# Two hops of graph attention on one Trainium2 core: the table work between the hops in several lots at once, and 64 gathers of the second hop moved there

## The reference

```python
def _hop(emb, head, tail, rel_e, W, N):
    a_input = jnp.concatenate([emb[head], emb[tail]], axis=-1)
    e = jnp.sum(a_input @ W * rel_e, axis=-1)
    e = jax.nn.leaky_relu(e, NEG_SLOPE)
    seg_max = jax.ops.segment_max(e, head, num_segments=N)
    ex = jnp.exp(e - seg_max[head])
    denom = jax.ops.segment_sum(ex, head, num_segments=N)
    alpha = ex / denom[head]
    agg = jax.ops.segment_sum(emb[tail] * alpha[:, None], head, num_segments=N)
    return agg + emb
...
for _ in range(N_HOPS):          # 2
    emb = _hop(emb, head, tail, rel_e, W, N)
    emb = emb / jnp.maximum(jnp.linalg.norm(emb, axis=-1, keepdims=True), 1e-12)
    res = 0.5 * res + emb
...
return _layernorm(x + res, axis=-1)
```

## Time and profile before

| | before |
|---|---|
| median of 3 runs | 5809.42 us (5805.15 to 5809.52) |
| profiled execution | 5806.54 us |
| its span, first to last instruction | 5804.8 us |
| granted TensorE clock, mean | 0.694 |
| busy: PE / DVE / ACT / POOL | 52% / 73% / 20% / 58% |
| sort and preparation | up to 1004 us |
| first hop's loop | 1004 to 3253 |
| stage between the hops | 3253 to 3447 |
| second hop's loop | 3447 to 5687 |
| last stage | 5687 to 5805 |

### The profile page before, as it was taken

The page is one execution under the profiler, slowest core; times in us unless marked ns, Lnnn a source line. Parts: engine busy times, 40 slices in busy tenths (PEclk is TensorE's granted clock), DMA queues, the critical chain, the costliest instruction groups (busy, mean ns, idle before and its releaser), DMA issues. The chain is left out here.

```text
span 5804.8 us, 102013 instructions
## 1 busy us (share of the span) xinstructions
PE 3025.6 (52%) x23525; PEld 2371.0 (41%) x23525; DVE 4227.0 (73%) x14510; ACT 1184.5 (20%) x4455; POOL 3349.3 (58%) x3535
## 2 busy tenths in 40 slices
PE   4411100566666665555666555656656656666661
PEld 1111100445544454444455324544545444454451
DVE  8899998677677776767767436777777677776777
ACT  3310000112222122121221331221212212122122
POOL 0000000777777777777777117777777777777770
PEclk9755555677677777777767557777777777777775
DMA  2000001222222222222222212222222222222223
GB/s 62 0 0 0 0 0 38 58 54 53 57 53 53 53 54 56 54 53 54 56 54 53 38 32 54 53 57 54 53 57 54 53 53 53 57 53 53 54 48 67
DMA packets 234922, 269.99 MB, mean 47 GB/s; under 512 B 140893, under 2 KB 149309, under 8 KB 234550
## 3 DMA queue, kind: packets, MB, share of 16 engines
q0 software_dynamic: 112640, 115.57, 10.2%
q1 hardware_dynamic: 121910, 151.13, 8.6%
HBM read 253.57 MB, written 12.88 MB: 46 GB/s over the span
## 5 line engine op out<-in xcount | busy, mean ns | idle before, releaser
L625 POOL DMA_INDIRECT G<-rows,ixs x3520 | 3343.3, 950 | 2301.7 <-DVE ixs L793 1229.6
L791 DVE SCALAR_TENSOR_TENSOR acc<-acc,aS,psY 65x128 f32 x3520 | 1206.7, 343 | 814.0 <-PE psY L689 553.8
L640 PE MATMUL psX<-PT,oht 128*128 x3532 | 945.7, 268 | 1240.1 <-DVE logit L752 1095.1
L689 PE MATMUL psY<-G,wr 128*65 128x128 f32 x7040 | 1305.4, 318 | 166.4 <-DVE acc L791 143.6
L752 DVE CUSTOM_DVE_ANT_0 junk<-psX,G 128x192 f32<-128x192 f32 x3520 | 1158.0, 346 | 276.0 <-DMA G<-rows,ixs 229.5
L640 PEld LDWEIGHTS psX<-PT,oht 128*128 128x128 bf16 x3532 | 411.5, 116 | 1523.0 <-issue 1507.6
L689 PEld LDWEIGHTS psY<-G,wr 128*65 128x65 f32 x7040 | 910.3, 165 | 257.7 <-issue 221.0
L643 PE MATMUL psX<-v2lo,oht 128*128 128x128 bf16 x3532 | 955.0, 270 | 0.0
L642 PE MATMUL psX<-v,oht 128*128 128x128 bf16 x3532 | 953.5, 270 | 0.0
L641 PE MATMUL psX<-PTlo,oht 128*128 x3532 | 933.8, 264 | 0.0
L716 ACT ACTIVATE wr<-G,wS 128x64 f32<-128x64 f32 x3520 | 863.0, 334 | 0.0
(11 more groups left out here) (165 smaller groups left out, 2186.8 us busy)
## 6 DMA issues: line engine op xcount, KB each, us to landing
tb<-types_lin SPq DMA_DIRECT2D x222, 512.0 KB
G<-rows,ixs POOLq DMA_INDIRECT x3520, 2.4
emb<-rows SPq DMA_DIRECT2D x14, 448.0 KB, 6.9
mt<-marks_d SPq DMA_DIRECT2D x110, 48.1 KB
rows<-xin SPq DMA_DIRECT2D x1, 3136.0 KB, 16.2
rows<-emb SPq DMA_DIRECT2D x14, 224.0 KB, 2.4
res<-rows SPq DMA_DIRECT2D x7, 448.0 KB, 6.9
out_dram<-res SPq DMA_DIRECT2D x13, 224.0 KB
```

The costliest lines, as they stand in the source:

```text
L625: nc.gpsimd.indirect_dma_start(G[:, p, u, L:L + D], None, tab[hop], bass.IndirectOffsetOnAxis(ap=ixs[:, p, u:u + 1], axis=0)).then_inc(gat ...
L640: nc.tensor.matmul(x[:, 0:L], piece, PT[:, bass.ds(first, L)], start=True, stop=False)
L689: nc.tensor.matmul(psY[:, v % 8, :], wr[:, v // 16, v % 16, :], G[:, pq, v, 0:L], start=True, stop=True).then_inc(y_ok, 1)
L791: nc.vector.scalar_tensor_tensor(spot, spot, aS[:, pq, v:v + 1], psY[:, v % 8, :], ALU.mult, ALU.add).then_inc(acc_ok, 1)
```

## The change

Five things change, all around the stage between the hops.

1. **Order of the table work.** Each lot's table work is cut into pieces (`turn`, `product`, `first`, `second`). A list, the same for PE and ACT, mixes the pieces of neighbouring lots: product t, turn t+1, second t-1, first t, and so on. Behind rows(0) to rows(2) comes no piece, behind a later rows(g) one (g divisible by 3) or two, and behind rows(13) all the rest. ACT does its share of the pieces of g behind square and root of lot g.
2. **Gathers between the hops.** POOL gets a program in this stage: when all 14 stores have landed, it issues the 64 gathers of the next hop's groups 0 and 1. DVE copies both groups' row numbers at the stage's start. In the second hop POOL starts at group 2.
3. **The nodes' rows lie in G.** G, `ixs` and `acc` are allocated once. The lots' old and new rows stand in columns 0 to 63 (lots 0 to 6) and 64 to 127 (lots 7 to 13) of G's 64 slots, so that the gathers can fill columns 128 to 191 beside them. `emb` is gone, and `res` exists in the last stage alone.
4. **Loads by single lots**: 224 KB each and a semaphore each, in both stages, instead of 448 KB for two lots.
5. **`acc` is cleared** for the second hop at the end of DVE's work in the stage between, no longer at the hop's front.

```diff
@@ the hop loop, POOL and DVE
-                        if not logits:
+                        if not logits or (hop and not reached(g, 2)):
                             return
...
-                        if logits:
+                        if logits and (not hop or reached(g, 1)):
                             nc.vector.tensor_copy(ixs[:, 1 - p, :], ix[:, bass.ds(CG * g + CG, CG)]).then_inc(ix_ok, 1)
...
-                    nc.vector.tensor_copy(ixs[:, 0, :], ix[:, 0:CG]).then_inc(ix_ok, 1)
+                    if not hop:
+                        nc.vector.tensor_copy(ixs[:, 0, :], ix[:, 0:CG]).then_inc(ix_ok, 1)
                     dve.wait_ge(cst, hop + 1)
                     nc.vector.memset(srow[:, :], NEG)
-                    link(nc.vector.memset(acc[:, :], 0.0))
+                    if not hop:
+                        link(nc.vector.memset(acc[:, :], 0.0))
@@ the stage on the nodes
+                spots = G[:, :, :, :].rearrange("l p u w -> l (p u) w")
+
+                def rows_of(b0, b1):
+                    assert b0 // (NB // 2) == (b1 - 1) // (NB // 2)
+                    side = b0 // (NB // 2)
+                    return spots[:, b0 - side * NB // 2:b1 - side * NB // 2, side * D:(side + 1) * D]
+
+                def lot(g):
+                    return rows_of(g * NG, (g + 1) * NG)
...
+                def table_work():
+                    order = [("turn", 0)]
+                    for t in range(NS + 1):
+                        if t < NS:
+                            order.append(("product", t))
+                        if t + 1 < NS:
+                            order.append(("turn", t + 1))
+                        if t:
+                            order.append(("second", t - 1))
+                        if t < NS:
+                            order.append(("first", t))
+                    at = 0
+                    for g in range(NS):
+                        n = 0 if g < 3 else (1 if g % 3 == 0 else 2)
+                        yield g, order[at:at + n]
+                        at += n
+                    yield NS, order[at:]
...
-                    for k in range(NS // 2):
-                        two = slice(2 * k * NG, 2 * (k + 1) * NG)
-                        sp.dma_start(emb[:, two, :], tv[:, two, :]).then_inc(e_in[k], 16)
+                    for g in range(NS):
+                        sp.dma_start(lot(g), tv[:, part(g), :]).then_inc(e_in[g], 16)
...
+                if not final:
+                    @block.gpsimd
+                    def _(gp):
+
+                        gp.wait_ge(ix_ok, NGRP + 3)
+                        gp.wait_ge(tabw, 16 * NS)
+                        for p in range(2):
+                            for u in range(CG):
+                                nc.gpsimd.indirect_dma_start(
+                                    G[:, p, u, L:L + D], None, tab[1], bass.IndirectOffsetOnAxis(ap=ixs[:, p, u:u + 1], axis=0)).then_inc(gath[p][u // 8], 16)
...
-                    for g in range(NS):
-                        rows(g)
-                        if not final and g >= 2:
-                            table(g - 2)
-                            first_off(g - 2)
-                            second_off(g - 2)
-                    if not final:
-                        for g in (NS - 2, NS - 1):
-                            table(g)
-                            first_off(g)
-                            second_off(g)
+                    if final:
+                        for g in range(NS):
+                            rows(g)
+                    else:
+                        for g, work in table_work():
+                            if g < NS:
+                                rows(g)
+                            for kind, t in work:
+                                {"turn": turn, "product": product, "first": first_off, "second": second_off}[kind](t)
...
+                        for g, work in table_work():
                             if g < NS:
-                                square(g, g, emb)
+                                square(g, lot(g))
                                 root(g, g, 1)
-                            if g > 1:
-                                tables_out(g - 2)
-                    if not final:
-                        tables_out(NS - 1)
+                            for kind, t in work:
+                                {"turn": turned_out, "product": high, "first": middle, "second": low}[kind](t)
...
+                    if not final:
+                        nc.vector.tensor_copy(ixs[:, :, :].rearrange("l p u -> l (p u)"), ix[:, 0:2 * CG]).then_inc(ix_ok, 2)
...
                             if g < NS:
                                 sum_up(g, g, 1.0, 1e-24, ALU.max)
+
+                        link(nc.vector.memset(acc[:, :], 0.0))
```

More of the change, by code:

```diff
@@ L494, in gnn_kernel @@
             "sc_ok", "y_ok", "acc_ok"))
-        e_in = [sem(f"e_in{k}") for k in range(NB // 14)]
+        e_in = [sem(f"e_in{k}") for k in range(NB // 7)]
         n_tr, nrow, nsq, nsum, nroot, rooted, e_new, T_new, eT_new, m_new, m2_new, m3_new, hi_new, mid_new, p_new, tabw, n_out, y_out = (sem(n) for n in (
@@ L501, in gnn_kernel @@
         hop_at = {"n": 0}
+        G = sb(ctx, "G", [L, 2, CG, L + D])
+        ixs = sb(ctx, "ixs", [L, 2, CG], i32)
+        acc = sb(ctx, "acc", [V, WIDE])
         USES = [-(-NGRP // 2), NGRP // 2]
@@ L833, in _ @@
                             sp.wait_ge(e_new, g + 1)
[L834 removed]
+                            sp.dma_start(tab[1].rearrange("(b p) d -> p b d", p=L)[:, part(g), :], lot(g)).then_inc(tabw, 16)
                         else:
@@ L853, in rows, with turn @@
                         last.then_inc(n_tr, 1)
-                    def table(g):
+                    halves = (slice(0, 4 * L), slice(4 * L, NG * L))
+                    def turn(g):
                         pe.wait_ge(e_new, g + 1)
@@ L873, in first_off @@
                         pe.wait_ge(hi_new, g + 1)
-                        for w in (slice(0, 4 * L), slice(4 * L, NG * L)):
+                        for w in halves:
                             last = nc.tensor.matmul(psQ[:, g % 2, w], lessb[:, :], PT[:, cols(g)][:, w], start=False, stop=True, skip_group_check=True)
@@ L909, in tables_out, with high, middle, low @@
                         nc.scalar.copy(eTn[:, g % 2, :, :], psE[:, 0:NG, :]).then_inc(eT_new, 1)
+                    def high(g):
                         act.wait_ge(m_new, g + 1)
                         nc.scalar.copy(PT[:, cols(g)], psQ[:, g % 2, 0:NG * L]).then_inc(hi_new, 1)
+                    def middle(g):
                         act.wait_ge(m2_new, g + 1)
+                        if g >= 2:
+                            act.wait_ge(m3_new, g - 1)
                         nc.scalar.copy(midn[:, g % 2, :], psQ[0:T, g % 2, 0:NG * L])
                         nc.scalar.copy(PT[T:2 * T, cols(g)], psQ[T:2 * T, g % 2, 0:NG * L]).then_inc(mid_new, 1)
+                    def low(g):
                         act.wait_ge(m3_new, g + 1)
                         nc.scalar.copy(PTlo[0:T, cols(g)], psQ[0:T, g % 2, 0:NG * L]).then_inc(p_new, 1)
-                    for g in range(NS + 1):
-                        if final:
+                    if final:
+                        for g in range(NS + 1):
                             if g:
-                                square(g - 1, lots0 + 2 * g - 1, res)
+                                square(lots0 + 2 * g - 1, res[:, part(g - 1), :])
                             if g < NS:
-                                square(g, lots0 + 2 * g, emb)
+                                square(lots0 + 2 * g, lot(g))
                             if g:
```

63 lines of the change are left out of this document (30 added, 33 removed).

## The result

| | before | after |
|---|---|---|
| median | 5808.11 us (4 runs, 5805.15 to 5809.52) | **5714.9 us** (4 runs, 5712.45 to 5716.19) |
| ratio | | 0.9843, 95% interval 0.9831 to 0.9855 |
| profiled execution, its span | 5806.54, 5804.8 | 5716.12, 5714.2 |
| granted TensorE clock, mean | 0.694 | 0.698 |

A forecast was written before the change was run, and what follows sets the result against it. GpSimd's unbroken gathers were taken to bound the kernel, so gather 65's start sets the time: 93.5 us earlier plus 2.2 in the last stage, 95.7 off 5806.5, plus 2.9 for the median, gives 5713 us; range 5695 to 5745.

The forecast's parts named there:

- leaving the stage: End of the stage between the hops: all engines meet 0.3 us after the last gather; 3 more if waiting for landing.
- types, to the one-hots: Second hop's start: VectorE's one-hots wait 5.0 us for the 512 KB of types, bounds 3.0 and 13.6.
- Rows first: Stage between hops: lots wait for fewer table pieces, bare ones 3.24 us; last new rows at 3316.9 instead of 3416.6.
- The tables' tail: 38 table pieces left after the rows: about 7.1 us a lot, ending at 3385, hidden by gathers with 15 us spare.
- 5733 rival: Tail of the tables does not overlap, each lot keeps 10.74 us, stage ends at 3420, 20 us later; chance 0.10.
- Rows that wait for the tables: Stage between hops: each lot stays at 13.52 us, gather 65 starts at 3535, no change, 5813; chance 0.03.
- Gathers that do not run early: Stage ends at 3385 and 64 gathers follow; gather 65 near 3466, 31 us later, 5744; chance 0.05.
- What the gathers run beside: 64 gathers between the hops, beside ScalarE's casts and the memset: priced at nothing; 10.6 us if the memset held them.
- 5702 case: Stage between hops: PE's clock rises to 2.4 GHz with closer-packed work, saving 11 us; chance 0.12.
- The steps set the rate: Second hop: each us a step exceeds 40.07 is paid by 53 groups; 5766 at 41.1; chances 0.05 to 41.9, 0.03 beyond.
- last step case: Second hop: steps of 42.3 us, a loss of 118 against the gain, 5835, slower than before; steps beyond 41.9 chance 0.03.
- The last stage: Last stage: loads halved from 448 KB to 224 KB, so VectorE waits 2.2 us less than 5.34.

The follow-up runs named there:

- e2_gathers_alone: Kernel after, but with the old order of table pieces, all four of lot g-2 behind rows(g): 5817.14 us, ratio to before 1.0017.
- e1_order_alone: Kernel after without GpSimd's program between the hops; the second hop gathers groups 0 and 1 itself: 5738.85 us, ratio to before 0.9877.
- e6_tables_last: Kernel after with no table piece between the rows, all 56 behind rows(13): 5705.18 us, ratio to before 0.9827.
- e5_clear_in_hop: Kernel after, but acc is cleared at the second hop's front again: 5725.12 us, ratio to before 0.9859.
- e4_forty: Kernel after with 40 gathers between the hops, the other 24 at the second hop's front: 5692.93 us, ratio to before 0.9801.
- e8_seven_of_eight: Kernel after without every eighth gather from group 2 of the second hop on, those slots keeping older rows: 5629.88 us, ratio 0.9696.
- e3_probe_end: Kernel after; behind its 64 gathers GpSimd writes a small tile, waits for all to land, writes another: 5717.32 us in one execution.
- e10_forty_late_exit: The kernel with 40 gathers between the hops; GpSimd then waits for the tables' last cast and writes one small tile: 5694.44 us, one execution.
- e7_write_only: Kernel after without gathers between the hops; GpSimd there waits for the tables' last cast and writes one small tile: 5733.05 us, one execution.
- e9_writes64: The kernel with one small write and no gathers between the hops, but with 64 one-element writes: 5738.86 us in one execution.

## Why the prediction was right, step by step

Gather 65 was put at 3435.0 and came at 3436.87. Term by term, measured less predicted, in us:

| term | measured | predicted | difference |
|---|---|---|---|
| lot 1 starts | 3259.16 | 3258.6 | +0.6 |
| lots 1 to 13 | 50.5 | 53.2 | -2.7 |
| lot 13 to the last new rows | 4.6 | 5.1 | -0.5 |
| landing of the stores, wake-up | 3.2 | 2.9 | +0.3 |
| 64 gathers | 79.6 | 80.1 | -0.5 |
| **leaving the stage** | **5.5** | **0.3** | **+5.2** |
| types, to the one-hots | 4.0 | 5.0 | -1.0 |
| step 0 | 17.5 | 17.6 | -0.1 |
| step 1, to gather 65 | 12.7 | 12.25 | +0.5 |
| sum | | | +1.8 |

- **The mechanism held.** Everything moved with gather 65, one for one, in all eleven kernels that keep the whole computation.
- **The mis-sized term** is "Leaving the stage": the 0.3 was given without a row; the moment beside it, from the earlier trace rows, is the end of a stage in which GpSimd had nothing to do, so it could not hold a price for leaving after gathers. The bound above it, 3 us for landing, was too low and named the wrong cause. That the time came out within 2 us is luck in part: the rows' phase and the types, 2.7 and 1.0 shorter than priced, paid back 3.7 of the 5.2.
- **Rows first.** The forecast form was right lot by lot, with each of these lots 0.3 to 0.75 shorter than priced: lot 4 took 6.95 (7.7), lot 5 5.0 (5.5), lot 8 7.0 (7.6), lot 10 5.6 (5.85), lot 11 3.3 (3.9).
- **The tables' tail** had its 15 us to spare: 16.6, at 6.91 a lot (7.1). The 5733 rival falls.
- **Two rivals were built.** Rows that wait for the tables (5813) are e2_gathers_alone, which took 5817.14: the 5.2 that leaving the stage took beyond its price are in it. Gathers that do not run early (5744) are e1_order_alone, 5738.85: its tables ended at 3377.75 and not at 3385.
- **What the gathers run beside** cost nothing: 64 in 79.6 us beside the memset and 46 instructions of ScalarE. The lock of VectorE and GpSimd on one port, which the Trainium skill states ("SBUF — State Buffer", Who interferes with whom), does not show in this memset's 10.62 us. That does not speak against the Trainium skill: for trn2 that section names `copy`, `cast` and `tensor_scalar` as the instructions with a two-port mode, and no memset, so the prediction's 10.6 us were a case that the rule does not claim.
- **The clock did not rise in the kernel after's trace.** Two windows of the kernel after (busy us (x count) of PE, PEld, DVE, ACT, POOL; PEclk, DMA share, GB/s), then two of e6_tables_last, where PE does nothing but tables:

```profile
3253.00:3317.00 64.00, 47.04 (x179) 26.39 (x180) 42.56 (x114) 32.73 (x54) 0.00 (x0) 0.50 0.50 101
3317.40:3397.30 79.90, 58.35 (x129) 21.00 (x128) 10.13 (x1) 40.34 (x46) 60.38 (x64) 0.50 0.14 26
```

```profile
3300.00:3340.00 40.00, 38.11 (x86) 14.88 (x88) 10.62 (x1) 24.84 (x28) 28.92 (x31) 0.50 0.13 29
3340.00:3383.00 43.00, 41.36 (x92) 15.80 (x92) 0.00 (x0) 27.58 (x31) 31.45 (x34) 0.50 0.12 26
```

  PE goes from 56% busy to 73%, in the last two windows to 95% and 96%, and the granted clock stays at 0.50, the 1.2 GHz level. So the 5702 case did not come. But the same table work can meet the other level: in e5_clear_in_hop the clock rose in the tail. Two windows of that run and its tables' last cast:

```profile
3300.00:3317.00 17.00, 15.57 (x52) 7.38 (x51) 11.62 (x31) 11.71 (x19) 0.00 (x0) 0.50 0.29 65
3324.00:3357.00 33.00, 26.67 (x109) 11.74 (x109) 0.00 (x0) 31.51 (x37) 24.82 (x27) 1.00 0.12 26
```

```profile
3361.95 0.90 ACT L968 CAST PTlo<-psQn 64x896 bf16<-64x896 f32 x1 [1.04 <-PE psQn L927]
```

  At 1.00, the 2.4 GHz level, a lot of the tail takes 4.51 us instead of 6.91, and the last cast ends at 3362.85 instead of 3380.44. It won nothing, as the gathers close that stage. In e1_order_alone and e4_forty the clock was 0.64 and 0.63 over 3275 to 3300, and lots 5 and 6 together took 7.45 instead of 8.23. The lift by activity that the Trainium skill states ("TensorE: Matmul & The Clock Gate", The HAM clock gate) is seen with these tables in e5_clear_in_hop, and not in the windows of the other two runs. In the 17 us ahead of 3317 PE was busy 15.57 us at 0.50 in the kernel after too, without the rise behind them; what decides between the levels no run here shows.
- **The steps set the rate**: it did not happen, as GpSimd has no wait above 0.3 in hop two but the first. But it was nearer than its 0.08 of chance said: step 1 alone gave 36.0, the steady step is 38.3 (e8_seven_of_eight), so 1.75 us are to spare. (The prediction's last step case adds up to 5713 + 118 = 5831, not 5835.) Why the steady step is 2.3 longer than step 1 was not traced.
- **GpSimd's rate**: 2.1 us lost over 1695 gathers, 1.2534 against 1.2521 each, without any long wait. Its cause was not traced.
- **The last stage** gave 1.1 where 2.2 was priced. VectorE's first wait there, in the timeline of the kernel after, is 3.13 against 5.34, as priced; the rest behind the last gather was longer by 1.1 us.

```profile
5603.67 0.63 DVE L1007 SCALAR_TENSOR_TENSOR res<-res,G 128x448 f32<-128x448 f32 x1 [3.13 <-DMA res<-rows]
```

- **The 2.9 us**, by which the median of before lay above its profiled execution, had no counterpart after: there the profiled execution, 5716.12, lies 1.2 above the median. Gather 65 (1.9 late), GpSimd's rate (2.1) and the last stage (1.1) put it 5.1 above the sum's 5710.8, within 0.2 of what was measured; in the medians 4.1 of these 5 us fell away. So it is luck in part, too, that 5713 and 5714.9 lie so close.

What stays open: what GpSimd does in the 5.5 us. The runs show that it comes behind GpSimd's last instruction, that it needs gathers in the stage, and that it is not their landing, 64 other instructions, or code being loaded. The trace shows no instruction in it.

## What to carry to other kernels

Where one engine issues without a hole, ask of a change only when its first unbroken issue starts, and follow that one moment through the stages. Work put into a gap is worth what still fits in front of the gap's other end: 64 gathers lost 10 us without the order, gained 24 with it, and 40 of them gained 46, since the tables close the gap when 40 are through; whether another number does better was not tried. A row taken from a block in which an engine did nothing gives no price for the block once the engine works in it. And a clock read in one trace holds for that execution: the same work met both levels here.

## What the runs showed of the hardware that was not expected

- Behind GpSimd's last instruction in a block in which it issued gathers, the next block starts late: 5.5 us after 64 of them (the kernel after; 5.5 also behind a wait for their landing, e3_probe_end), 3.6 after 40, even with 13.4 us of idling in between (e10_forty_late_exit); 0.3 after one small write or 64 (e7_write_only, e9_writes64).
- The granted clock of the same table work differed from one execution to another: 0.50 over 83 us with PE 95% and 96% busy in e6_tables_last, 1.00 over 33 us in e5_clear_in_hop, where a lot took 4.51 us instead of 6.91.
- The memset of acc starts 2.58 or 2.59 us after the instruction before it in every place that it was put, behind other VectorE work and at a hop's front alike (3316.91 in the kernel after, 3406.50 in e5_clear_in_hop, and the earlier trace rows).
